# Attention value products taken two steps at a time in a written-out order, and the split of a block's maxima moved from VectorE to GpSimd

## The reference, cut to what matters

```python
q, k, v = (xn @ W.T, split into 16 heads of 16)      # q and k with rotary angles
scores = einsum('bhqd,bhkd->bhqk', q, k) / 4         # causal: later keys are masked
attn = softmax(scores, axis=-1)
out = einsum('bhqk,bhkd->bhqd', attn, v) @ Wo.T
ffn = fp4_linear(silu(fp4_linear(xn, w_gate)) * fp4_linear(xn, w_up), w_down)   # 704 inner
```

## Time and profile before

| | |
|---|---|
| median of 3 executions | 2763.79 us (2763.39 to 2765.77) |
| profiled execution | 2764.13 us, of which the span of the trace 2762.3 us |
| granted TensorE clock over the span | 0.971 |
| PE busy | 2568.4 us, 93% |
| DVE busy | 2335.1 us, 85% |
| ACT busy | 1656.0 us, 60% |
| POOL busy | 16.0 us, 1% |
| DMA | 157.84 MB, mean 57 GB/s |

### The profile page before, as it was taken

The page is one execution under the profiler, slowest core; times in us unless marked ns, Lnnn a source line. Parts: engine busy times, 40 slices in busy tenths (PEclk is TensorE's granted clock), DMA queues, the critical chain, the costliest instruction groups (busy, mean ns, idle before and its releaser), DMA issues. The chain is left out here.

```text
span 2762.3 us, 55520 instructions
## 1 busy us (share of the span) xinstructions
PE 2568.4 (93%) x14690; PEld 1163.9 (42%) x14690; DVE 2335.1 (85%) x5197; ACT 1656.0 (60%) x3323; POOL 16.0 (1%) x7
## 2 busy tenths in 40 slices
PE   3699999999996899999999999999999999999979
PEld 2355556565553233333333333333333333333337
DVE  7889898888996888888898888888988988889803
ACT  2354544545542277777777767777777777667762
POOL 0000000000002000000000000000000000000000
PEclk8899999999997699999999999999999999999999
DMA  5111211112112301202111112011011111110017
GB/s 177 37 62 68 68 68 58 58 67 68 68 61 78 94 27 53 60 26 57 33 46 58 31 46 63 27 52 60 26 57 33 46 58 31 46 57 5 7 30 218
DMA packets 174761, 157.84 MB, mean 57 GB/s; under 512 B 53360, under 2 KB 153456, under 8 KB 174576
## 3 DMA queue, kind: packets, MB, share of 16 engines
q1 hardware_dynamic: 174576, 155.39, 18.3%
HBM read 95.81 MB, written 58.72 MB: 56 GB/s over the span
## 5 line engine op out<-in xcount | busy, mean ns | idle before, releaser
L1081 ACT ACTIVATE prob<-score 128x512 f32<-128x512 f32 (+3 forms) x2560 | 1189.6, 538 | 555.9 <-PE score L1017 313.0
L1125 DVE TENSOR_REDUCE top<-tile 128x1 f32<-128x512 f32 x1536 | 969.0, 684 | 116.7 <-PE tile L989 110.7
L989 PE MATMUL tile<-ks,qs 96*128 96x512 bf16 (+3 forms) x2560 | 852.3, 357 | 36.9 <-POOL ks L1105 20.8
L1012 PE MATMUL score<-qs,ks 99*128 99x512 bf16 (+3 forms) x2560 | 815.8, 350 | 19.8 <-ACT prob L1081 10.0
L1032 PE MATMUL acc<-prob,vs 128*32 128x512 f32 (+3 forms) x5120 | 600.2, 541 | 0.4 <-ACT prob L1081 0.4
L1130 DVE CUSTOM_DVE_ANT_0 tile<-tile,mask 128x128 f32<-128x128 f32 (+3 forms) x1024 | 473.0, 522 | 68.8 <-PE tile L989 63.4
L989 PEld LDWEIGHTS tile<-ks,qs 96*128 96x128 bf16 x2560 | 239.2, 98 | 536.5 <-DVE top L1125 207.8
L1012 PEld LDWEIGHTS score<-qs,ks 99*128 99x128 bf16 x2560 | 248.1, 98 | 369.7 <-ACT prob L1081 260.9
L360 PE MATMUL gu<-wguT,xT 128*128 128x512 f32 (+1 forms) x768 | 313.8, 562 | 20.7 <-DVE hid L668 20.7
L1017 PE MATMUL score<-identb,maskb 128*128 128x128 bf16 x1024 | 214.3, 221 | 3.2 <-issue 3.2
L360 PEld LDWEIGHTS gu<-wguT,xT 128*128 128x128 f32 x768 | 144.7, 192 | 167.6 <-issue 124.5
(11 more groups left out here) (101 smaller groups left out, 1746.8 us busy)
## 6 DMA issues: line engine op xcount, KB each, us to landing
qkp<-parts SPq DMA_DIRECT2D x192, 128.0 KB
qs<-qkp SPq DMA_DIRECT2D x384, 64.0 KB, 2.6
ks<-qkp SPq DMA_DIRECT2D x384, 64.0 KB, 2.5
vscr<-vt SPq DMA_DIRECT2D x16, 1024.0 KB, 4.5
vs<-vscr SPq DMA_DIRECT2D x16, 1024.0 KB, 6.2
x_all<-in_x SPq DMA_DIRECT2D x16, 512.0 KB, 8.9
oscr<-ot SPq DMA_DIRECT2D x64, 128.0 KB, 1.7
att<-oscr SPq DMA_DIRECT2D x64, 128.0 KB, 2.6
```

What stands on the lines that cost most here:

```text
L989: mm = nc.tensor.matmul(bank[:, h * width:(h + 1) * width], qs[par][0:ROWS, h0 + h, q0:q0 + P], ks[par][0:ROWS, h0 + h, k0:k0 + width], st ...
L1012: mm = nc.tensor.matmul(bank[:, 0:width], ks[par][0:ROWS_M, h, kb * P:(kb + 1) * P], qs[par][0:ROWS_M, h, qb * GROUP + off:(qb + 1) * GROU ...
L1081: nc.scalar.activation(prob[:, k % PROB_SLOTS, 0:width], score[:, k % SCORE_SLOTS, 0:width], ACT.Exp, scale=HEAD ** -0.5).then_inc(probs_r ...
L1125: nc.vector.tensor_reduce(top[:, j, h0, c:c + 1], bank, AX.X, ALU.max).then_inc(tile_taken, 1)
```

## The change

- `prob` gets room for 4 steps and not 2 (`PROB_STEPS`), and the weighs come in pairs: ahead of the fourth score block of every even step n both step n-2 and step n-1 are weighed. The last pair stands at the end of the iteration. The matching semaphore counts go from 2 to `PROB_STEPS`. In the list `scores` the weighs are entries like score blocks.
- The rule that spread the tiles is replaced by a string, `ORDER`: "s" takes the next of `scores` (a score block or a weigh), "t" the next tile, "r" a row, "o" an out. A "top" follows its last tile at once.
- Of the maxima, DVE keeps the reduction (and then waits for it to be done). The two copies and the two subtractions move to GpSimd (`split_maxima`), each waiting for the one before, in the same order over the plan. DVE waits, before it writes `topm` again, until the split before is done.

The long strings are whole, the removed rule is cut.

```diff
@@ -54,10 +54,11 @@
 OT = GT * OUTW
 LEAD = 0.52
-TOP_APART, OUT_APART = 6, 3
-LAST_TILES = 4
-WEIGH_AT = 3
-MASK_WEIGHT = 1.5
+WEIGH_AT, WEIGH_STEPS = 3, 2
+ORDER = ("stsststtsttssststststsssstststsstssrtsssttstssotststsstsststststtstsststssststststssttsstsssstst"
+         "stsststsssststssttsotsststsstttsststsststttsstsssststsstttststssssststststssttsssstrtstssttstsst"
+         "stsssstssttstssssrtsssttstsststsoststsststststtsststtstsssstsstststttssssssstststtrsststsssststs"
+         "ttssttstsstssstsstttstsststssststsstststtststsssssstttssssto")
 
 class Chain:
@@ -761,48 +762,33 @@
     steps = [(qb, kb, kb - 4 * qb if kb >= 4 * qb else None) for qb in range(QB) for kb in range(4 * qb + 4)]
-    weight = [GT if j is None else GT - j + MASK_WEIGHT for _, _, j in steps]
...
+    scores = []
+    for n, (qb, kb, j) in enumerate(steps):
+        for h in range(HG):
+            if h == WEIGH_AT and n and n % WEIGH_STEPS == 0:
+                scores += [("weigh", m, *steps[m]) for m in range(n - WEIGH_STEPS, n)]
+            scores.append(("scores", HG * n + h, n, qb, kb, j))
+    scores += [("weigh", m, *steps[m]) for m in range(n + 1 - WEIGH_STEPS, n + 1)]
+
+
+    plan, rows, outs, scored, at = [], [], 0, 0, 0
+    for letter in ORDER:
+        if letter == "s":
+            plan.append(scores[scored])
+            scored += 1
+        elif letter == "o":
+            plan.append(("out", outs))
+            outs += 1
+        elif letter == "r":
             plan.append(rows.pop(0))
...
-        units = [[("scores", HG * n + h, n, qb, kb, j)] for h in range(HG)]
-        if n:
-            units.insert(WEIGH_AT, [("weigh", n - 1, *steps[n - 1])])
+        else:
+            plan.append(events[at])
+            at += 1
+            if at < len(events) and events[at][0] == "top":
+                rows.append(("row", *events[at][1:]))
+                plan.append(events[at])
+                at += 1
+    assert scored == len(scores) and at == len(events) and outs == QB and not rows
     for qb in range(QB):
         start = next(n for n, e in enumerate(plan) if e[0] == "scores" and e[3] == qb)
@@ -831,7 +817,8 @@
     plan, STEPS = attention_plan()
     HEAD_STEPS = HG * STEPS
-    SCORE_SLOTS, TILE_SLOTS, PROB_SLOTS = 3, 4, 2 * HG
+    SCORE_SLOTS, TILE_SLOTS, PROB_STEPS = 3, 4, 2 * WEIGH_STEPS
+    PROB_SLOTS = PROB_STEPS * HG
     ROW_COLS, ROW_LANDS = HG * PARTS * GT, HG * 16
     ahead_places = {e: n for n, e in enumerate(e for e in plan if e[0] in ("tile", "row") and e[-1])}
     places = {more: ring_places(plan, more) for more in (True, False)}
@@ -888,7 +875,10 @@
         dve_passed = sem("dve_passed")
         row_landed = [sem(f"row_landed{c}") for c in range(QB)]
         dve_links = sem("dve_links")
+        topm_ready = sem("topm_ready")
         top_ready = sem("top_ready")
+        pool_links = sem("pool_links")
+        pool_passed = sem("pool_passed")
         out_stored = [sem("out_stored0"), sem("out_stored1")]
         sp_passed = sem("sp_passed2")
         block = ctx.enter_context(nc.Block())
@@ -954,7 +944,7 @@
                             stack(ks[par], 1, TERMS_K, it + 2, kb // GT, k_loaded[par][kb // GT])
                 if more is True:
-                    await_on(sp, sp_passed, pv_done, it * STEPS + STEPS + 2)
+                    await_on(sp, sp_passed, pv_done, it * STEPS + STEPS + PROB_STEPS)
                     v_load(par, it + 2)
             with loop(nc, sp, ITERS // 2 - 1) as i:
@@ -1082,7 +1072,7 @@
                                      ACT.Exp, scale=HEAD ** -0.5).then_inc(probs_ready, 1)
             def take_acc(it, e):
-                act.wait_ge(pv_done, it * STEPS + e[1] + 1 + 2)
+                act.wait_ge(pv_done, it * STEPS + e[1] + 1 + PROB_STEPS)
                 nc.scalar.copy(acc_sb[:], acc[:]).then_inc(acc_taken, 1)
             def iteration(it):
@@ -1098,16 +1088,44 @@
         @block.gpsimd
         def _(pool):
-            for s, n in ((probs_ready, SCORE_SLOTS), (pv_done, 2), (acc_taken, 1), (tile_taken, TILE_SLOTS),
+            for s, n in ((probs_ready, SCORE_SLOTS), (pv_done, PROB_STEPS), (acc_taken, 1), (tile_taken, TILE_SLOTS),
                          (out_stored[0], 1), (out_stored[1], 1)):
                 pool.sem_inc(s, n)
             for par in range(2):
                 nc.gpsimd.memset(ks[par][ROWS:P, :, :], 1.0).then_inc(consts_ready, 1)
+            TOP_LINKS = 3
+
+            def split_maxima(number, qb):
+
+                part = top_parts[:, qb, 0:ROW_COLS].rearrange("q (h p j) -> q j h p", p=PARTS, j=GT)
+                m, r = (a[:].rearrange("p (j h) -> p j h", h=HG) for a in (topm, rest))
+                done = number * TOP_LINKS
+                await_on(pool, pool_passed, topm_ready, number + 1)
+                nc.gpsimd.tensor_copy(part[:, :, :, 0], m).then_inc(pool_links, 1)
+                await_on(pool, pool_passed, pool_links, done + 1)
+                nc.gpsimd.tensor_tensor(r, m, part[:, :, :, 0], ALU.subtract).then_inc(pool_links, 1)
+                await_on(pool, pool_passed, pool_links, done + 2)
+                nc.gpsimd.tensor_copy(part[:, :, :, 1], r).then_inc(pool_links, 1)
+                await_on(pool, pool_passed, pool_links, done + 3)
+                nc.gpsimd.tensor_tensor(part[:, :, :, 2], r, part[:, :, :, 1], ALU.subtract).then_inc(top_ready, 1)
+
+            def iteration(it, more):
+                for e in plan:
+                    if e[0] == "top" and (more or not e[-1]):
+                        split_maxima((it + e[2]) * QB + e[1], e[1])
+
+            for e in plan:
+                if e[0] == "top" and e[-1]:
+                    split_maxima(e[1], e[1])
+            with loop(nc, pool, ITERS - 1) as it:
+                iteration(it, True)
+            iteration(ITERS - 1, False)
+
         @block.vector
         def _(dve):
             link = Chain(dve, dve_links)
-            TOP_LINKS, OUT_LINKS = 4 * QB, QB
+            OUT_LINKS = QB
             nc.vector.memset(top_parts[:, :, ROW_COLS:P], 0.0).then_inc(consts_ready, 1)
             nc.vector.tensor_copy(identb[:], identf[:]).then_inc(consts_ready, 1)
             dve.wait_ge(mask_loaded, 16)
@@ -1132,18 +1150,16 @@
                         scale=1.0, scalar=MASK, op0=ALU.add, op1=ALU.max, accum_out=top[:, j, h0 + h, c:c + 1])
                 last.then_inc(tile_taken, 1)
-            def maxima(it, more, qb):
+            def maxima(it, more, number, qb):
                 n, _ = place(it, more, last_tile[qb])
                 dve.wait_ge(tile_taken, n + 1 + TILE_SLOTS)
-                part = top_parts[:, qb, 0:ROW_COLS].rearrange("q (h p j) -> q j h p", p=PARTS, j=GT)
-                m, r = (a[:].rearrange("p (j h) -> p j h", h=HG) for a in (topm, rest))
-                link(nc.vector.tensor_reduce(topm[:], top[:, :, :, 0:qb + 1].rearrange("p j h c -> p (j h) c"),
-                                             AX.X, ALU.max, negate=True))
-                link(nc.vector.tensor_copy(part[:, :, :, 0], m))
-                link(nc.vector.tensor_tensor(r, m, part[:, :, :, 0], ALU.subtract))
-                link(nc.vector.tensor_copy(part[:, :, :, 1], r))
-                nc.vector.tensor_tensor(part[:, :, :, 2], r, part[:, :, :, 1], ALU.subtract).then_inc(top_ready, 1)
+                if it is not None or qb:
+
+                    dve.wait_ge(top_ready, number)
+                nc.vector.tensor_reduce(topm[:], top[:, :, :, 0:qb + 1].rearrange("p j h c -> p (j h) c"),
+                                        AX.X, ALU.max, negate=True).then_inc(topm_ready, 1)
+                dve.wait_ge(topm_ready, number + 1)
             def take_row(it, more, e):
                 nc.vector.tensor_copy(row[:, e[1], :], tile_bank(it, more, e)[0:ROW_COLS, 0:P]).then_inc(tile_taken, 1)
...
```

More of the change, by code:

```diff
@@ L762, in attention_plan @@
     steps = [(qb, kb, kb - 4 * qb if kb >= 4 * qb else None) for qb in range(QB) for kb in range(4 * qb + 4)]
-    weight = [GT if j is None else GT - j + MASK_WEIGHT for _, _, j in steps]
[L765 to L780, removed]
-            plan.append(rows.pop(0))
@@ L783, in attention_plan @@
-    for n, (qb, kb, j) in enumerate(steps):
-        units = [[("scores", HG * n + h, n, qb, kb, j)] for h in range(HG)]
-        if n:
-            units.insert(WEIGH_AT, [("weigh", n - 1, *steps[n - 1])])
[L787 to L805, removed]
+    scores = []
[4 more added lines that the diff above has]
+            scores.append(("scores", HG * n + h, n, qb, kb, j))
@@ L1166, in _ @@
                 elif e[0] == "top" and e[-1]:
-                    maxima(None, None, e[1])
+                    maxima(None, None, e[1], e[1])
                 elif e[0] == "row" and e[-1]:
                     take_row(None, None, e)
-            links_ahead = link.n
+            assert not link.n
             def iteration(it, more):
-                link.enter(it * (TOP_LINKS + OUT_LINKS) + links_ahead)
+                link.enter(it * OUT_LINKS)
```

(4 more changed lines are left out.)

## The result

| | before | after |
|---|---|---|
| median, runs | 2764.44 us, 4 (2763.39 to 2765.77) | 2681.49 us, 4 (2678.93 to 2684.88) |
| ratio of the two | | 0.9699, 95% interval 0.9688 to 0.9711 |
| profiled execution, its span | 2764.13, 2762.3 us | 2682.65, 2680.5 us |
| mean of iterations 2 to 13 of attention | 108.54 us | 102.66 us |

The change is 3.0% faster. 2688 had been forecast, with a range of 2658 to 2728.

What follows compares the result with a forecast made beforehand. PE was taken as the bound. An iteration of 99.6 us plus gaps 1.1, end 1.2, ACT 0.7 and DVE 0.9 made 103.5 against 108.65; 15 x 5.1 = 76.5 off 2764.1 gave 2688 us, range 2658 to 2728.

Steps and rivals of the forecast that it cites:

- PE is the bound: In one attention iteration PE's spacings sum to 103.0 of 108.65 us; the other 5.6 are waits and small gaps.
- A pair saves 0.18: A second weigh right behind the first saves 0.18 us, in 19 of 20 pairs: 3.4 us an iteration.
- What pairs ask of ACT, 0.7: Behind pairs followed by 6 tiles ACT's exponentials come 0.15 to 0.25 us late; over all stretches 0.7 us an iteration.
- The order at the end, 1.2 stays: At an iteration's end the out's wait grows from 0.41 to some 0.6 us, the last pair's shrinks; 1.2 stay.
- Less work on DVE, 0.9 of waits left, the split worth 1 to 1.5: DVE loses 3.2 us of work an iteration; PE's waits for it fall from 2.4 to about 0.9 us.
- GpSimd hidden, a link of 0.4: The four split operations on GpSimd take about 0.4 us each, 1.6 in all, hidden ahead of PE's row.
- rival D: PE's row waits for slow GpSimd links; from 1.37 us a link the kernel is slower, at 1.80 2843 us; chance 0.07.
- two warnings: GpSimd's two-input elementwise work is about twice as slow as VectorE's; a freshly loaded kernel's first call costs about 6 us.
- Row of block 3, nothing: Block 3's row has 6.4 us of PE work to land in, needs 5.8 to 6.7: taken as 0, at most 0.3.
- The last iteration, a pair 5.2: In its tile-free part a pair of steps takes 5.2 us, not 4.80, +3 in all; its first half offsets that.
- The sum: An iteration of 103.5 us against 108.65, 5.1 less, times 15: 76.5 us saved, giving 2688 us.
- rival A: PE's waits only move: all 5.6 us stay, the gain is 2.7 us an iteration, 2724 us; chance 0.16.

Runs made afterwards that it cites:

- every combination: The eight kernels with old or written order, single or paired weighs, split on VectorE or GpSimd, before and after included: 2681.5 to 2774.9 us.
- the experiment above: Changed kernel with single weighs from step 20 in the last iteration, plus one tile moved behind each iteration's last weigh: 2678.08 us.

## Why the prediction was right, step by step

*PE is the bound:* right; the sum of spacings held in every combination (small gaps 1.1 to 1.55), but for the stretches at the lower clock in two of the kernels.

*A pair saves 0.18:* right in kind, 0.05 too small. It is 0.23, of which 0.03 is the break between halves that I had kept inside the pair and that isn't there, and 0.02 was lost to two-digit rows. 19 x 0.23 = 4.4 for my 3.4. That is the mis-sized term. The Trainium skill (TensorEngine Tiling (Array Packing), section "Key Properties") says that changing the tiling mode drains the engine; the trace agrees, with 0.09 on the way in, 0.12 on the way out, and nothing between steps of one mode. The outs, float32 but of full width, have no break, which bears it out.

*What pairs ask of ACT, 0.7:* about right. Waits at score blocks after the change are 1.0, of which 0.2 on average is the loop's end; before 1.5. That pairs also cost DVE's slots, I had only as part of the DVE term: in the written order 1.15 us of waits for tile slots exist with pairs and not without.

*The order at the end, 1.2 stays:* right, the out waits 0.63 where I said 0.6 (0.85 from the tile's start, less 0.22). With one tile more in front of it, in the experiment above, it is 0.40, as before the change.

*Less work on DVE, 0.9 of waits left, the split worth 1 to 1.5:* 1.25 left, worth 1.8.

*GpSimd hidden, a link of 0.4:* right, 0.40 to 0.44. The slacks I gave, 3.1, 3.7, 4.5, 7.6 behind the reduction, were 3.2, 3.5, 3.8 and 5.4; 3 links more (1.2) used none of them up, 8 links more used up three. The rival D was real as a mechanism and far away, and its price above the threshold is one for one as the prediction had it, with the falls of the clock, which it didn't have, on top.

Neither of the two warnings that the prediction took from the Trainium skill (GPSIMD Engine Reference, sections "Performance versus the Vector engine" and "Architecture") shows: the subtractions took 0.23 and 0.27 against 0.19 and 0.23 on DVE, and the first call, at 893.83, took 0.25 as all later ones, 0.17 behind the end of the reduction that it waits for, again as all later ones. A whole link, though, took 1.8 times DVE's, near the estimate of 0.5.

*Row of block 3, nothing:* right, no wait for its DMA after the start.

*The last iteration, a pair 5.2:* right, 5.22, though five pairs stand there whole and not seven. The sum's 0 for the iteration was near: from its first score block to its last out it is 0.8 shorter.

*The sum:* 76.5 foreseen, 81.5 in the profiled executions (81.8 in their spans). From first out to first out, 5.9 in each of 13 iterations are 76.6, the 14th, at the loop's exit, gives 5.2, the 15th only 2.3; the time up to the first out gives 1.4, the last iteration's outs take 2.3 back and the output projection 1.4. In the 15th DVE stands idle 2.07 us, the last 1.2 of them with a full tile before it, PE then 1.65 for it, and the clock falls to 1.2 GHz for 3.4 us. What held DVE there the trace doesn't show. The other profiles show that it goes with the split: DVE stands for 2.07 to 2.84 at that place in all nine kernels that have it on GpSimd, and in none of the four that have it on VectorE. In the old kernel with only the split moved this iteration is 2.1 longer than before, all others 1.3 or more shorter. So the move has a price, once in the kernel, that the prediction put at nothing.

*Against rival A* (the waits only move): the range held it at 2724. The old rule with pairs shows that it was no idle worry: there waits ate all that the breaks gave.

## What to carry to other kernels

Where matmuls of two array forms alternate, each way in and out costs a fixed time (here 0.21 together), so group the work of one form; but a longer group starves the engines that feed and drain PE, and pays in full only with the rest of the order rewritten around it and the tightest of those engines relieved: here +0.7, -0.5, -2.5 or -3.5 us an iteration for the same edit. Small chains that one engine needs late can go to an idle, slower engine as long as their slack is read from the trace (last producer to first consumer); beyond it, each microsecond costs one. When a stall costs more than its own length, look at the granted clock before blaming other engines: start to start, slow matmuls look like waits, and only their durations and the clock tell them apart. In a stretch where another engine sets the pace the grouping costs (here 0.4 a pair in the trace).

## What the runs showed of the hardware that I had not expected

GpSimd's small operations (128 x 16, float32 and bf16) took 0.23 to 0.27 us, against 0.19 to 0.23 on VectorE, and a dependent link 0.40 to 0.44 against 0.22 to 0.24: most of the difference is the wait between (0.17 to 0.18), not the operation. With three waits of PE of 1.2 to 1.8 us in each iteration, the granted clock fell to 1.2 GHz for 3.4 us once in nearly every iteration, at 1.6 us each; with none above 0.5 it stayed at 2.4 GHz from 946.7 us to the loop's exit. At the start of the loop's unrolled rest PE stood 2.8 to 3.4 us with nothing to wait for in the trace, in all 13 kernels at the same matmul, and the clock fell for 3.4 or 6.8 us; some 37 to 41 us later DVE stood for 2.07 or more in the nine that have the split on GpSimd.
